# A graph network kernel on one core: twenty places gathered by single edges, slots unpacked in odd row counts, VectorE's loops written out

## The reference

```python
deg = jnp.maximum(segment_sum(ones, dst), 1.0);  d = deg ** -0.5
h = relu(layernorm(x))
feat = h
for i in range(10):                       # ten hops
    agg = segment_sum(feat[src] * (d[dst] * d[src])[:, None], dst)
    feat = (agg * 0.9 + 0.1 * h) * reg[i] + (1.0 - reg[i]) * feat
x = x + feat
e = relu(layernorm(x))
for _ in range(4):                        # four message-passing steps
    m = (e @ W_msg.T + b_msg).reshape(3125, 4, 128)
    r = segment_sum(m[src, edge_type], dst)
    e = gru_cell(r, e)
return x + e
```

## Time and profile before

| | |
|---|---|
| median of 3 runs | 2251.09 us (2250.48 to 2251.97) |
| the profiled execution's own time | 2250.78 us |
| its span, first to last instruction | 2248.9 us |
| mean granted TensorE clock | 0.928 of full |
| busy in the span | TensorE 92%, VectorE 60%, GpSimd 39%, ScalarE 22% |

### The profile page before, as it was taken

How to read it: one execution, slowest core, us unless ns; L and a number is a source line. 1 busy time by engine, 2 the same in 40 slices (tenths; PEclk the granted TensorE clock), 3 DMA queues, 4 the chain that set the end, 5 groups by cost and what they waited for, 6 DMA issues and landing times.

```text
span 2248.9 us, 42235 instructions
## 1 busy us (share of the span) xinstructions
PE 2064.0 (92%) x15410; PEld 1443.1 (64%) x16017; DVE 1346.0 (60%) x2875; ACT 495.3 (22%) x1130; POOL 885.8 (39%) x1022
## 2 busy tenths in 40 slices
PE   3666665899999999999899999999999999999998
PEld 2333333899989988898655576555765557655576
DVE  8999998777777778786842236422354223553233
ACT  4989887200000000000210002100022000220001
POOL 4978773000000000000058860488604886048870
PEclk9555555899999999999999999999999999999999
DMA  2000000000000000002431111311103111033111
GB/s 83 24 35 35 24 35 36 30 1 2 1 2 2 2 1 2 1 1 91 145 93 42 42 34 40 99 41 42 36 23 113 41 43 37 24 112 70 41 39 31
DMA packets 62730, 89.73 MB, mean 40 GB/s; under 512 B 31953, under 2 KB 48927, under 8 KB 59654
## 3 DMA queue, kind: packets, MB, share of 16 engines
q1 hardware_dynamic: 21185, 54.88, 7.4%
q0 software_dynamic: 38400, 31.28, 6.0%
q10 hardware_dynamic: 2944, 0.93, 0.2%
HBM read 47.48 MB, written 39.05 MB: 38 GB/s over the span
## 4 chain that ended last, share of the span: by engine, by line
PE 75%; DVE 16%; issue 4%; DVEq 3%; ACT 2%; POOL 0%; POOLq 0%; DMA 0%; ACTq 0%
PE ps L912 39%; PE ps L1016 28%; PE ps L895 4%; DVE marks L1218 3%; DVEq L1205 2%; DVE m_full L1688 2%; DVE m_parts L1681 2%; DVE weighed L1223 1%; PE ps L926 1%; DVE dig L1246 1%; DVE big L1248 1%; PE ps L875 1%; PE ps L837 1%; PE ps L1001 1%; DVE hot_pair L1220 1%
## 5 line engine op out<-in xcount | busy, mean ns | idle before, releaser
L508 POOL DMA_INDIRECT big<-messages_by_edge_kind,edge_row x480 | 616.6, 1285 | 1156.7 <-issue 876.2
L912 PE MATMUL ps<-slots,m_parts 125*128 125x436 fp8e4 (+1 forms) x5600 | 960.8, 330 | 4.5 <-DVE m_parts L1681 3.2
L912 PEld LDWEIGHTS ps<-slots,m_parts 125*128 125x128 f16 x5600 | 539.9, 98 | 360.6
L1016 PE MATMUL ps<-parts,big 125*128 125x256 f16 x6125 | 669.0, 273 | 1.1 <-DVEq L1630 1.1
L1016 PEld LDWEIGHTS ps<-parts,big 125*128 125x128 fp8e4 x6125 | 590.7, 98 | 64.1
L1519 DVE TENSOR_SCALAR slots<-big 128x1400 int32<-128x1400 int32 (+1 forms) x224 | 196.5, 920 | 259.5 <-PE ps L912 241.3
L793 PE MATMUL ps<-hot_pair,weighed 125*128 125x228 f16 x1000 | 219.5, 372 | 118.4 <-ACT weighed L621 73.1
L793 PEld LDWEIGHTS ps<-hot_pair,weighed 125*128 125x128 f16 x1000 | 118.0, 124 | 219.8 <-ACT weighed L621 181.3
L621 ACT ACTIVATE weighed<-marks,win_w 125x128 f16<-125x128 f16 x625 | 194.5, 390 | 40.7 <-DVE marks L1218 40.7
L560 ACT ACTIVATE rs<-rs 125x25 f32<-125x25 f32 (+3 forms) x5 | 1.1, 216 | 697.5 <-DVE rs L1088 697.5
L1708 DVE SCALAR_TENSOR_TENSOR gate_r<-ps,over,gate_r 128x436 f32<-128x436 f32 (+2 forms) x32 | 20.0, 624 | 213.6 <-PE ps L895 169.6
(11 more groups left out here) (231 smaller groups left out, 1553.2 us busy)
## 6 DMA issues: line engine op xcount, KB each, us to landing
messages_by_edge_kind<-m_parts SPq DMA_DIRECT2D x20, 1120.0 KB
packed_counts<-packed SPq DMA_DIRECT2D x16, 625.0 KB, 2.9
big<-messages_by_edge_kind,edge_row POOLq DMA_INDIRECT x480
big<-packed_counts SPq DMA_DIRECT2D x4, 1400.0 KB, 6.4
big<-packed_counts SPq DMA_DIRECT2D x3, 1050.0 KB, 5.8
messages_by_edge_kind<-m_parts SPq DMA_DIRECT2D x20, 130.0 KB
hd<-in_x SPq DMA_DIRECT2D x1, 1562.5 KB
x_again<-in_x SPq DMA_DIRECT2D x1, 1562.5 KB
```

Source lines behind the costliest of these rows:

```text
L508: pool.indirect_dma_start(out=picked[0:CH, r, w, :, :].rearrange("p h f -> p (h f)"), out_offset=None, in_=m_dram[:, :], in_offset=bass.In ...
L912: last = pe.matmul(ps[:, k % 2, 0:SIZES[k] * QD], m_parts[0:Q, a, t, h, :], slots_f8[0:Q, t % 2, 0:SIZES[k], a, 0:QD], start=a == 0 and t ...
L1016: last = pe.matmul(ps[:, n % RING, 0:2 * F], tot_f8[0:Q, c, a, :], both((parts0, parts1)[par], a), start=a == 0, stop=a == TILES - 1)
```

## The change

- `QD` goes from 109 to 105, so 20 places (500 targets) are picked and the dense matmuls are 420 and 315 columns wide. The stride of a row stays at 2800 bytes.
- The picked edges are the last 17,125 edges of the list, 137 gathers of 125 (the last lot has two). Each gather has a window of 40 targets at a base that is fixed in the program (`BASES`); the edges' targets, sources and types are loaded from DRAM one word to a partition (three loads on SP's queue behind x), `late_edges` works out rows and windows once, before the last two `sum_digits`, and sets a flag if an edge falls outside its window. A matmul of zeros over 500 columns opens bank 6, and the picked matmuls have 40 columns. GpSimd's 24 small copies, VectorE's pair windows and `edge_parts` go; seven `mark_targets` stand beside hop 7 in place of eight beside hop 8.
- The lots are spread anew (28, the last three at (6, 0)), the last store of messages is split into three and two tiles, and the picked turn's sum is taken on ScalarE in the picked turn and on VectorE after block 5's update.
- `unpack` works over rows (0, 3) and (3, 4) in blocks of four and over (0, 3) in blocks of three.
- VectorE's two loops, over hops 0 to 5 and over the first three steps, are written out.

```diff
-QD = 109
+QD = 105
-GW = 15
-PC = 2 * TILES
-PAIRS = (Q - QD) // 2
+GE = 125
+GATHERS = 137
+FIRST_EDGE = E - GATHERS * GE
+PC = 40
+PICKED = TILES * (Q - QD)
+BASES = [min(max(BASE_AT + 19 * (j // BASE_STEP) + 4 * (j % BASE_STEP), 0), PICKED - PC) for j in range(GATHERS)]
...
-LOTS_AT = {(1, 0): (0, 1), (1, 1): (2,), (1, 2): (3,), (1, 3): (4, 5), (2, 0): (6,), (2, 1): (7,), (2, 2): (8, 9), (2, 3): (10,),
-           (3, 0): (11, 12), (3, 1): (13,), (3, 2): (14,), (3, 3): (15,), (4, 0): (16, 17), (4, 1): (18,), (4, 3): (19, 20),
-           (5, 0): (21,), (5, 1): (22,), (5, 2): (23,)}
+LOTS_AT = {(1, 0): (0, 1), (1, 1): (2, 3), (1, 2): (4,), (1, 3): (5,), (2, 0): (6, 7), (2, 1): (8,), (2, 2): (9,), (2, 3): (10, 11), (3, 0): (12,), (3, 1): (13, 14), (3, 2): (15,), (3, 3): (16,), (4, 0): (17,), (4, 1): (18,), (4, 2): (19,), (4, 3): (20,), (5, 0): (21, 22), (5, 1): (23,), (5, 3): (24,), (6, 0): (25, 26, 27)}
-STORED = [(0, 5), (5, 10), (10, 15), (15, 20), (20, 25)]
+STORED = [(0, 5), (5, 10), (10, 15), (15, 20), (20, 23), (23, 25)]
...
             sp.dma_start(hd[0:Q, :, :].rearrange("p c f -> p (c f)"), x_v).then_inc(s_x, 16)
+            with nc.allow_non_contiguous_dma("last edges, one to a partition"):
+                for to, a in ((late_target, dst), (edge_row, src), (late_type, edge_type)):
+                    sp.dma_start(to[0:GE, :], a[FIRST_EDGE:E].rearrange("(j p) -> p j", p=GE)).then_inc(s_late, 16)
...
+                if lot == 0:
+                    pe.matmul(ps[:, 6, 0:PICKED], zeros[0:GE, :], hot_room[0:GE, 0:PICKED].bitcast(F8), start=True, stop=False, skip_group_check=True)
...
-                        last = pe.matmul(ps[:, 6, pair * PC:(pair + 1) * PC], picked[0:CH, r, w, h, :], hot_to_f8[0:CH, pair, first + w, :],
+                        last = pe.matmul(ps[:, 6, BASES[at]:BASES[at] + PC], picked[0:GE, r, w, h, :], hot_to_f8[0:GE, at, :],
...
+            def late_edges():
+
+                at = slice(0, GATHERS)
+                rel, base, low = late_rel[0:GE, at], late_base[0:GE, at], late_low[0:GE, at]
+                target, kind, within, row = late_target[0:GE, :], late_type[0:GE, :], win_to[0:GE, :], edge_row[0:GE, :]
+                dve.wait_ge(s_late, 48)
+                step(TS(base, base, 0.0, float(PICKED - PC), ALU.max, ALU.min))
+                step(TS(rel, target, -float(TILES * QD), None, ALU.add))
+                step(TT(within, rel, base, ALU.subtract))
+                step(TS(low, within, 0.0, None, ALU.is_lt))
...
+                STT(out=row, in0=row, scalar=float(TYPES), in1=kind, op0=ALU.mult, op1=ALU.add).then_inc(s_rows, 1)
...
             for q in range(BQ * (NB - 1), Q):
                 onehots(q, q % DEPTH, q % WINDOWS)
+            late_edges()
             sum_digits(NB - 2, 0)
...
-                for lo, hi in ((0, size // 2), (size // 2, size)):
+                for lo, hi in ((0, 3), (3, size))[:size - 2]:
...
-                with dve.Fori(0, HOPS // 2 - 2) as i:
-                    steps.loop(i, 2 * (1 + 5 * TILES))
-                    for par in range(2):
-                        hop(2 * i + par, par, TILES * (2 * i + par))
-                steps.done(HOPS // 2 - 2)
-                for h, beside in ((HOPS - 4, scales_beside), (HOPS - 3, edges_beside), (HOPS - 2, targets_beside)):
+                for h in range(HOPS - 4):
+                    hop(h, h % 2, TILES * h)
+                for h, beside in ((HOPS - 4, scales_beside), (HOPS - 3, targets_beside), (HOPS - 2, None)):
...
-                            if after[0] == "picked":
-                                sum_low(turn + 1, picked_sums(after[1]), picked_parts(after[1], u + 1, 1), picked_parts(after[1], u + 1, 0))
...
                     dve.sem_inc(s_emb, 1)
+                    if after and after[0] == "picked":
+                        sum_low(turn + 1, picked_sums(after[1]), picked_parts(after[1], u + 1, 1), picked_parts(after[1], u + 1, 0))
...
-                with dve.Fori(0, STEPS - 1) as s:
-                    steps.loop(s, 4 * TURNS)
-                    gnn_step(s, True)
-                steps.done(STEPS - 1)
-                gnn_step(STEPS - 1, False)
+                for s in range(STEPS):
+                    gnn_step(s, s < STEPS - 1)
```

More of the change, by code:

```diff
@@ L90, with shelf_rows @@
 WD = W - WA
+def shelf_rows(lot):
+    return sum(LOT_SIZE[n % LOTS] for n in range(lot % SHELVES, lot + 1, SHELVES))
 class Chain:
@@ L503, in _ @@
                     for lot in range(LOTS):
-                        r = lot % SHELVES
-                        pool.wait_ge(s_got_used[r], USES * s + lot // SHELVES + 1)
-                        for w in range(LOT):
+                        turn, r = divmod(LOTS * s + lot, SHELVES)
+                        pool.wait_ge(s_got_used[r], turn + 1)
+                        for w in range(LOT_SIZE[lot]):
                             at = lot * LOT + w
                             pool.indirect_dma_start(
-                                out=picked[0:CH, r, w, :, :].rearrange("p h f -> p (h f)"), out_offset=None, in_=m_dram[:, :],
-                                in_offset=bass.IndirectOffsetOnAxis(ap=edge_row[0:CH, at:at + 1], axis=0)).then_inc(s_got[r], 16)
+                                out=picked[0:GE, r, w, :, :].rearrange("p h f -> p (h f)"), out_offset=None, in_=m_dram[:, :],
+                                in_offset=bass.IndirectOffsetOnAxis(ap=edge_row[0:GE, at:at + 1], axis=0)).then_inc(s_got[r], 16)
             with pool.If(over_any > 0):
@@ L840, in _ @@
             pe.wait_ge(s_flag, 1)
-            pe.matmul(ps[0:1, 7, 0:1], over1[0:Q, 0:1], onesf[0:Q, 0:1], start=True, stop=True).then_inc(s_flagp, 1)
+            pe.matmul(ps[0:1, 7, 0:1], over1[0:Q, 0:1], onesf[0:Q, 0:1], start=True, stop=False)
+            pe.matmul(ps[0:1, 7, 0:1], over1[0:GE, 2:3], onesf[0:GE, 0:1], start=False, stop=True).then_inc(s_flagp, 1)
             pe.wait_ge(s_flagi, 1)
@@ L1175, in _ @@
             dve.wait_ge(s_win_row, 1)
-            begins, ends = (windows[0:1, j * QB + QD:j * QB + Q].rearrange("o (g two) -> o g two", two=2) for j in (0, 2))
-            TT(pair_lo[0:1, :], begins[:, :, 0], begins[:, :, 1], ALU.min)
-            step(TT(pair_hi[0:1, :], ends[:, :, 0], ends[:, :, 1], ALU.max))
-            dve.sem_inc(s_pair, 1)
-            step(TT(pair_span[0:1, :], pair_hi[0:1, :], pair_lo[0:1, :], ALU.subtract))
-            step(dve.tensor_reduce(over1[0:1, 1:2], pair_span[0:1, :], AX.X, ALU.max))
-            step(TS(over1[0:1, 1:2], over1[0:1, 1:2], GW + 0.5, None, ALU.is_gt))
+            step(dve.tensor_reduce(over1[0:1, 1:2], windows[0:1, QD:Q], AX.X, ALU.min))
+            step(TS(over1[0:1, 1:2], over1[0:1, 1:2], (FIRST_EDGE + CH - 1) // CH - 0.5, None, ALU.is_lt))
             dve.sem_inc(s_prep, 1)
@@ L1250, in sum_digits @@
                 dve.sem_inc(s_digits, 1)
+            def late_edges():
[7 more added lines that the diff above has]
+                step(TS(low, within, 0.0, None, ALU.is_lt))
+                step(STT(out=low, in0=rel, scalar=0.0, in1=low, op0=ALU.is_ge, op1=ALU.mult))
+                step(STT(out=low, in0=within, scalar=PC - 0.5, in1=low, op0=ALU.is_gt, op1=ALU.add))
+                step(dve.tensor_reduce(over1[0:GE, 2:3], low, AX.X, ALU.add))
+                step(TS(over1[0:GE, 2:3], over1[0:GE, 2:3], -4.0, None, ALU.mult))
+                STT(out=row, in0=row, scalar=float(TYPES), in1=kind, op0=ALU.mult, op1=ALU.add).then_inc(s_rows, 1)
             def onehots_general(n, q, b, m):
```

103 lines of the change are left out of this document (36 added, 67 removed).

## The result

| | before | after |
|---|---|---|
| median | 2251.16 us (4 runs, 2250.48 to 2251.97) | 2233.57 us (4 runs, 2233.26 to 2233.77) |
| profiled execution, its span | 2250.78, 2248.9 us | 2233.26, 2231.3 us |

The ratio is 0.9922, with an interval of 0.9904 to 0.9939: 17.6 us faster, where 26.0 were forecast. The direction came as forecast, and so did the larger terms; some 8 us of the gain are missing. The time lies inside the 80% range (2214 to 2250), but at the upper edge of what the forecast itself allowed (2217 to 2233).

A forecast was written before the change was run, and what follows sets the result against it. TensorE was taken as the bound, with VectorE on the chain around step changes. Terms -30.9 - 2.2 - 2.2 - 1.0 + 0 + 10.3 = -26.0 us took 2251.1 to 2225 us; 80% range 2214 to 2250.

The forecast's parts named there:

- The dense matmuls: TensorE's dense matmuls outside the messages, narrowed from 109 to 105 places, save 0.420 ns a column: -30.9 us.
- Narrower matmuls among the messages and the loops: 400 narrower matmuls among the messages, mostly paid: -2.2 us; VectorE's loop written out over three steps: another -2.2 us.
- Unpacking: VectorE's three-row unpacks run at the slow pace; seven bare ones cost 1.47 us each: +10.3 us.
- The gathers: GpSimd's 137 gathers a step finish about 1 us before TensorE needs the last lot: 0 us.
- The rival in which they bind: Gathers keep 1.59 us each and bound the kernel, 8 us a step, 2257 us; chance 0.05, 0.03 for part.
- The picked sum moved, and the nine small instructions: Moved sum on ScalarE and VectorE: 0, at most +0.5 us a step; late_edges' VectorE instructions covered, +2 us if not.
- The word loads: Three loads on SP's queue at the start: 0 us; rival that they stall stores: mild 0.10, hard 0.15.
- The picked matmuls: 274 matmuls of 40 columns a step plus an opening one cost what the old lots did: 0 us, at most +4.4.
- The gates beside them: Gates beside the picked matmuls keep 3125 columns a step; wider and narrower pieces cancel: 0 us.
- The hops' loop: VectorE's hops loop written out removes TensorE's wait at the end of a loop pass: -1 us at most.

The follow-up runs named there:

- experiment 7: The kernel before with VectorE's two loops (hops and steps) written out and nothing else changed: 2248.47 us, ratio 0.9987.
- experiment 3: The changed kernel with VectorE's two loops (hops and steps) put back: 2250.87 us, ratio 0.9999 against the kernel before.
- Experiment 2: The changed kernel with even-half unpacks only for slots 1 and 2 of each step's first block, odd rows elsewhere: 2224.39 us, ratio 0.9879 against the kernel before.
- Experiment 1: The changed kernel with every unpack split in even halves again: 2261.83 us, ratio 1.0051 against the kernel before.
- experiment 4: The changed kernel with each picked matmul over only the first 20 of its 40 columns: 2233.66 us, ratio 0.9924 against the kernel before.
- experiment 8's fastest version: The kernel of Experiment 2 with the next step's slot 1 unpacked after the two bias sums: 2220.04 us, ratio 0.9859 against the kernel before.

## Why the prediction came out as it did

**The dense matmuls** (-30.9): right. Pieces of fifty are 0.33 and 0.25 us shorter, 56 x 0.33 + 48 x 0.25 = 30.5 us.

**Narrower matmuls among the messages and the loops** (-2.2 and -2.2): right. For the loops the waits for m_parts, which fell by 2.2 us, and experiment 7 show it; for the narrower matmuls only the rows do, since no run takes them alone. What the prediction didn't see is that the loops' price depends on the rest of the kernel: with them back (experiment 3) the whole gain is gone. The term's size holds against the kernel before; against the changed kernel with its loops it is 17.3 us, which no row ahead of the change showed.

**Unpacking** (+10.3): right. 2.335 us for 2100 elements, 6.0 us more for slots and 4.0 for messages, 10.0 in all. Experiment 2, with the fast pace at these two places, is 9.2 us faster.

**The gathers** (0, with about 1 us to spare): right. Experiment 1 shows the price of the other case, +28 us, of which some 10 are TensorE's clock. The rival in which they bind was built on the right pace, 1.59 us, which came with the even halves and not with the odd ones.

**The picked sum moved, and the nine small instructions** (0 and 0): right. TensorE waits for r_parts once, 0.5 us, in both kernels, and 11.7 us at the end of counting (385 us) in both.

**The word loads** (0): right in the result, with the pace close: from about 30 to 94 us for 10,275 words on each of five engines would be 6.2 ns, against 5.9 from the bias words and 7.1 as the limit. How many engines took part is less sure: the DMA share was 0.46, more than the five that were counted.

**The picked matmuls** (0): this is the step that failed. "Ten columns less at the same slope make 20.8 ns" was a slope read between 327 and 436 columns and used at 40. The gap between dense pieces held 25 ns a matmul at 50 columns, hardly more than the 24 ns that experiment 4 finds at 20. The upper bound, 40 columns at the price of 50, was the truth. In the chain of step 0 the picked matmuls take 7.04 us (274) where they took 6.24 (240), and the opening one 0.21: 1.01 us a step, **+4.0 us**. The gates beside them, seven pieces of 18 that were also counted as nothing, take 21.77 us for 21.64, +0.5 in all.

**The hops' loop** (-1): nothing came. TensorE's wait for VectorE's queue there is 1.2 us for 1.1, and the hops start at 424.37 in place of 423.90 us.

**TensorE's clock** (not counted): +1.7 us in the profiled execution. The second step is 1.66 us longer than its neighbours. TensorE's rows there and the windows say why:

```profile
1671.62 1.12 PE L882 MATMUL ps<-w_parts,emb_parts 128*125 128x512 f16 x3 [2.08 <-DVE m_full L1668]
1672.53 1.61 PE L919 MATMUL ps<-slots,m_parts 125*128 125x420 fp8e4 x4
1673.93 1.49 PE L882 MATMUL ps<-w_parts,emb_parts 128*125 128x512 f16 x3
1675.21 1.00 PE L919 MATMUL ps<-slots,m_parts 125*128 125x420 fp8e4 x4
1676.05 0.81 PE L882 MATMUL ps<-w_parts,emb_parts 128*125 128x512 f16 x3
```

```profile
1672.50:1674.50 2.00, 2.00 (x7) 0.50 0.06 21
```

Behind the waits of 1.11 and 2.08 us the granted clock is 0.50 (1.2 GHz, the lower of its two levels) until about 1675 us. Two rounds of a message and four dense matmuls, 1.37 us each elsewhere, take 2.31 and 2.12 there, 1.7 us more. The other steps have the same two waits and no fall. No such fall stands in the steps of the kernel before or of experiment 7, whose waits for messages at the changes of step are 1.8 to 1.9 us. (Ahead of the steps, among the first six messages, both kernels have one, at about 1099 us.) There is one in the steps of the profiled executions of experiments 2 (behind a wait of 1.93 us) and 4, both at another step, and none in experiment 8's fastest version, where that wait is 0.76 us. From experiment 2 to that version the profiled spans differ by 4.9 us: the waits for messages give 3.5, those for rows 0.8, the fall that is missing 1.7, and three short idles take 0.7 back. That the shorter wait is why the clock stayed up is likely and not shown.

The sum by these readings is -30.5 - 2.7 (columns among the messages, 400 x 6.7 ns) - 2.2 + 4.0 + 0.5 + 10.0 + 1.7 + 0.5 (the later hops) = -18.7 us, against -17.6 in the spans; about 1 us is not traced to a row. Against the forecast of -26.0, picked matmuls and gates, hops' loop and clock make up 4.5 + 1.5 + 1.7 = 7.7 of the 8.4 us.

Left open: why the loops cost so much more in the changed kernel (experiment 3 alone shows a stall with packets of instructions behind it), and what beside a wait decides whether the clock falls; neither has a run that takes the one cause alone.

## What to carry to other kernels

A slower instruction can be the better one where the faster one holds up a neighbour (gathers of 1217 ns beside unpacks in odd rows, 1284 beside even halves): look for where it stands bare and use the fast form there and only there. Don't carry a slope per column down to sizes that no row shows; the gap that the small matmuls leave between large ones is their price. Time an edit in the kernel where it will live: writing the loops out was worth 3.3 us in one version and 17.3 in the other. Keep a list of what a change has just enough of (here the gathers' last lot, the stores behind the loads, VectorE's 1.32 us against TensorE's 1.37): the runs above took away each of them, and it cost from 2 us (the pace) to 52 us (the loads).

## What the runs showed of the hardware that was not expected

- A jump back on VectorE cost 6.40 us twice, with packets of instructions landing behind it; in the kernel before, the same loop shows no gap and 0.7 us of longer waits a pass.
- The same instructions with their waits take 1.41 us a pair inside a loop and 1.32 written out.
- Three loads of 17,125 single words each held the queue for some 64 us, 1.2 ns a word, and the stores issued behind them landed only then.
- TensorE's granted clock fell to 0.50 behind a wait of about 2 us in some steps and not in others of the same execution, and one such fall cost 1.7 us; in experiment 1 it fell in seven stretches behind waits for rows.
